# Value products and contexts on 58 columns, maxima transposed in half precision, logits copied four at a time

## The reference

```
h = layernorm(concat(emb[x], window3(pca[x]) @ proj) @ fus)
a = layernorm(h)
q, k, v = a @ Wq, a @ Wk, a @ Wv             # 16 heads of 64, biases
ctx = softmax(q k^T / 8) v
h = h + layernorm(a + ctx @ Wo + bo)
x = layernorm(h); scores = softmax(x @ wg + bg)    # 16 experts
# top 2 of 16 experts per token; per expert the best 64 of 128 positions
h = h + layernorm(x + sum_e scatter(gelu(x_e @ w1_e + b1_e) @ w2_e + b2_e))
```

## Time and profile before

| | us |
|---|---|
| median of 3 runs | 556.43 (555.6 to 559.4) |
| the profiled execution | 557.69 |
| its span, first to last instruction | 555.7 |
| TensorE busy in the span | 516.9 (93%) |
| VectorE busy | 448.6 (81%) |
| GpSimd busy | 382.2 (69%) |
| ScalarE busy | 367.2 (66%) |

### The profile page before, as it was taken

One profiled execution on the slowest core, in us unless ns is written; L12 is line 12 of the kernel. 1 busy time (PEld: TensorE's weight loads), 2 busy tenths in 40 slices (PEclk: granted clock), 3 DMA queues, 4 the chain that ended last, 5 costly groups with the idle time before them and its releaser, 6 DMA issues. The chain is left out here.

```text
span 555.7 us, 16203 instructions
## 1 busy us (share of the span) xinstructions
PE 516.9 (93%) x6063; PEld 385.9 (69%) x6063; DVE 448.6 (81%) x1013; ACT 367.2 (66%) x776; POOL 382.2 (69%) x508
## 2 busy tenths in 40 slices
PE   4996879999999999999999999878999999999874
PEld 2894757777777777777777777643457676676664
DVE  5676668888888988888888888977976988887775
ACT  1588668787877878787778778616675555555440
POOL 4000876787878878787878788942177887898783
PEclk9997999999999999999999999999999999999999
DMA  6900000000000000000000000000733044172011
GB/s 195 351 4 0 2 2 3 4 3 1 4 3 2 4 3 2 4 4 2 4 3 4 2 3 2 3 0 2 156 87 86 21 122 104 23 170 54 28 40 58
DMA packets 11905, 21.74 MB, mean 39 GB/s; under 512 B 4668, under 2 KB 9780, under 8 KB 10164
## 3 DMA queue, kind: packets, MB, share of 16 engines
q1 hardware_dynamic: 11828, 20.71, 13.6%
HBM read 16.24 MB, written 4.33 MB: 37 GB/s over the span
## 5 line engine op out<-in xcount | busy, mean ns | idle before, releaser
L792 POOL TENSOR_TENSOR s_pl<-s_pf,s_ph 128x512 f16<-128x512 f32 x128 | 147.0, 1159 | 6.9 <-ACT s_ph L890 6.7
L979 DVE TENSOR_REDUCE s_mx<-ps 128x4 f32<-128x512 f32 x128 | 83.7, 676 | 29.0 <-PE ps L1120 28.9
L770 PE MATMUL ps<-s_xt_all,s_w1s 128*128 128x512 f16 x384 | 87.8, 379 | 2.2 <-ACT s_ub L1432 1.6
L1587 PE MATMUL ps<-s_w2s,s_hid 128*128 128x256 f16 x768 | 88.9, 273 | 0.0
L884 ACT ACTIVATE s_pf<-ps 128x512 f32<-128x512 f32 x128 | 76.6, 601 | 17.3 <-PE ps L1133 17.2
L1587 PEld LDWEIGHTS ps<-s_w2s,s_hid 128*128 128x128 f16 x768 | 75.1, 98 | 10.9
L890 ACT ACTIVATE s_ph<-s_pf 128x512 f16<-128x512 f32 x128 | 77.2, 637 | 0.0
L1166 PE MATMUL ps<-s_zh,s_cth 128*128 128x256 f16 x256 | 69.8, 273 | 0.0
L1166 PE MATMUL ps<-s_zh,s_ctl 128*128 128x256 f16 x256 | 69.8, 273 | 0.0
L1166 PE MATMUL ps<-s_zl,s_cth 128*128 128x256 f16 x256 | 69.8, 273 | 0.0
L770 PEld LDWEIGHTS ps<-s_xt_all,s_w1s 128*128 128x128 f16 x384 | 37.4, 98 | 41.5 <-ACT s_ub L1432 2.1
(11 more groups left out here) (231 smaller groups left out, 1241.3 us busy)
## 6 DMA issues: line engine op xcount, KB each, us to landing
s_rep<-picks SPq DMA_DIRECT2D x14, 512.0 KB, 6.1
s_stage<-in_w SPq DMA_DIRECT2D x2, 1024.0 KB, 13.8
out<-s_ot_a SPq DMA_DIRECT2D x16, 128.0 KB, 1.7
out<-s_lg SPq DMA_DIRECT2D x16, 128.0 KB, 1.7
s_stage<-in_wq SPq DMA_DIRECT2D x1, 1024.0 KB, 5.0
s_stage<-in_wk SPq DMA_DIRECT2D x1, 1024.0 KB, 6.6
s_stage<-in_wv SPq DMA_DIRECT2D x1, 1024.0 KB, 8.3
s_stage<-in_wo SPq DMA_DIRECT2D x1, 1024.0 KB, 10.0
```

The source lines that it names most:

```text
L770: mm = nc.tensor.matmul(hidden_bank(n)[:], w1s[:, wp, c, j * P:(j + 1) * P], xt_all[:, GB * g:GB * (g + 1), xp, c, :], start=(k == 0), sto ...
L792: nc.gpsimd.tensor_tensor(flat(pl[:, b % 2, 4 * j:4 * j + 4, :]), pf[:, j, :], flat(ph[:, b % 2, 4 * j:4 * j + 4, :]), ALU.subtract).then_ ...
L979: nc.vector.tensor_reduce(mx[:, b % 2, c:c + 4], A[ab][:].rearrange("p (h k) -> p h k", h=4), AX.X, ALU.max).then_inc(max_done[hf][ab], 1)
L1587: mm = nc.tensor.matmul(zb[b % 4], hid[:, g % 2, hp, j, t * P:(t + 1) * P], w2s[:, wp, j, :], start=False, stop=(j == NJ - 1 and hp == 1))
```

## The change

- `values` multiplies only UV = 58 columns of `u` (0 to 57); `context` reads and writes only those. The six pad columns of `cn` for each head are set to zero once by VectorE, at the head of its program in this block, and TensorE's first `turn` waits for it (`cn_zero`).
- `mx` is f16, and `maxima_cols` is a matmul of f16 `mx` with an f16 identity in place of an fp32 transposition. The f16 identity, until now freed after the first block, is kept.
- `logits` of sequence b go to columns 256 + 16 (b % 4) of MISC, and `logits_out` copies the 64 columns of four sequences in the steps with i % 4 == 2. `x_cols` and `maxima_cols` wait for `lg_done` only once in four sequences.

```diff
@@ -40,6 +40,7 @@
 NJ = E * FP // P
 UD = 64
 R2, ONE, SHIFT = 2 * V, 2 * V + 1, 2 * V + 2
+UV = ONE + 1
 GB = 4
 NG = B // GB
 TAKE = S // 2
@@ -99,7 +100,7 @@
         tok = sb("h", [P, B, D])
         mvx = sb("mvx", [P, B, 2])
         lg = sb("lg", [P, B, E])
-        ident = sb("ident", [P, P])
+        ident, identh = sb("ident", [P, P]), sb("identh", [P, P], F16)
         ga1_b, ga2_b, be2_b = (sb(n, [P, D]) for n in ("ga1_b", "ga2_b", "be2_b"))
         bg_b = sb("bg_b", [P, E])
         w1s = sb("w1s", [P, 2, KC, E * FP], F16)
@@ -138,7 +139,7 @@
         ids_i, mask_i = sb1("ids_i", [P, B], I32), sb1("mask_i", [P, B], I32)
         ids_f, mask_f = sb1("ids_f", [P, B]), sb1("mask_f", [P, B])
         band, iota = sb1("band", [P, P]), sb1("iota", [P, V])
-        band16, ident16, identh = sb1("band16", [P, P], BF16), sb1("ident16", [P, P], BF16), sb1("identh", [P, P], F16)
+        band16, ident16 = sb1("band16", [P, P], BF16), sb1("ident16", [P, P], BF16)
         lhs_t = sb1("lhs_t", [P, 2 * KC, UD])
         pcaT, proj_w, proj_bT = sb1("pcaT", [20, V]), sb1("proj_w", [20, D]), sb1("proj_bT", [P, KC])
         fus_w, fus_b = sb1("fus_w", [P, 2 * KC, D]), sb1("fus_b", [1, D])
@@ -706,7 +707,7 @@
         qh, ql = sb2("qh", [P, 2, 2, 4, P], F16), sb2("ql", [P, 2, 2, 4, P], F16)
         pf = sb2("pf", [P, 4, 512])
         ph, pl = sb2("ph", [P, 2, H, P], F16), sb2("pl", [P, 2, H, P], F16)
-        mx = sb2("mx", [P, 2, H])
+        mx = sb2("mx", [P, 2, H], F16)
         mrow = sb2("mrow", [H, 2, P], F16)
         rsum = sb2("rsum", [P, 2, 8])
         cn = sb2("cn", [P, 2, 4, P])
@@ -723,7 +724,7 @@
         def sems(name, n):
             return [sem(f"{name}{k}") for k in range(n)]
 
-        rows_ready, w_hi = sem("rows_ready"), sem("w_hi")
+        rows_ready, w_hi, cn_zero = (sem(n) for n in ("rows_ready", "w_hi", "cn_zero"))
         tok_done = sems("tok_done", 3)
         shift_in = sems("shift_in", 2)
         q_ready, qhi_done, qlo_done, sm_ready, st_ready = (
@@ -988,9 +989,9 @@
                     dve.wait_ge(rs_done[hf], b + 1)
                     if b >= 1:
                         dve.wait_ge(t_ready[hf], b)
-                    nc.vector.tensor_tensor(cn[:, hf].rearrange("p t (a u) -> p (t a) u", u=UD),
-                                            CB[hf][:].rearrange("p (h u) -> p h u", u=UD),
-                                            rsum[:, hf].rearrange("p (h o) -> p h o", o=1).to_broadcast([P, 8, UD]),
+                    nc.vector.tensor_tensor(cn[:, hf].rearrange("p t (a u) -> p (t a) u", u=UD)[:, :, 0:UV],
+                                            CB[hf][:].rearrange("p (h u) -> p h u", u=UD)[:, :, 0:UV],
+                                            rsum[:, hf].rearrange("p (h o) -> p h o", o=1).to_broadcast([P, 8, UV]),
                                             ALU.mult).then_inc(cn_done[hf], 1)
 
                 def context_lo(b, hf):
@@ -1020,9 +1021,10 @@
                     nc.vector.tensor_tensor(xt_all[:, b, 1].rearrange("p c t -> p (c t)"), MISC[:, 0:D],
                                             xt_all[:, b, 0].rearrange("p c t -> p (c t)"), ALU.subtract).then_inc(xlo_done, 1)
 
-                def logits_out(b):
-                    dve.wait_ge(lg_ready, b + 1)
-                    nc.vector.tensor_scalar(lg[:, b, :], MISC[:, D:D + E], 1.0 / W_SCALE, None, ALU.mult).then_inc(lg_done, 1)
+                def logits_out(g):
+                    dve.wait_ge(lg_ready, 4 * g + 4)
+                    nc.vector.tensor_scalar(both(lg[:, 4 * g:4 * g + 4, :]), MISC[:, D:D + 4 * E], 1.0 / W_SCALE, None, ALU.mult)\
+                        .then_inc(lg_done, 1)
 
                 def token_rows(n):
                     dve.wait_ge(rows_ready, n + 1)
@@ -1033,6 +1035,7 @@
 
                 DVE_TOKENS = {(-5, 0): (2,), (-5, 1): (5,), (-5, 2): (8,), (-4, 0): (11,), (-4, 1): (14,)}
 
+                nc.vector.memset(cn[:].rearrange("p h t (a u) -> p (h t a) u", u=UD)[:, :, UV:UD], 0.0).then_inc(cn_zero, 1)
                 for i in STEPS:
                     if has(i + 5):
                         q_lo(i + 5, 1)
@@ -1061,8 +1064,8 @@
                         gate_part(dve, 2 * i - 53, early)
                     if has(i + 3):
                         sum_root(i + 3, 1)
-                    if has(i + 1):
-                        logits_out(i + 1)
+                    if has(i + 1) and i % 4 == 2:
+                        logits_out((i + 1) // 4)
                     if has(i + 2):
                         y_scaled(i + 2)
                     if has(i + 3):
@@ -1147,11 +1150,13 @@
                             c = (2 * t + ab) * UD
                             h = 8 * hf + 4 * ab + t
                             for n, (p, u) in enumerate(((ph, uh), (ph, ul), (pl, uh))):
-                                mm = nc.tensor.matmul(CB[hf][:, c:c + UD], p[:, b % 2, h, :], u[:, b, 0, :],
+                                mm = nc.tensor.matmul(CB[hf][:, c:c + UV], p[:, b % 2, h, :], u[:, b, 0, 0:UV],
                                                       start=(n == 0), stop=(n == 2))
                     mm.then_inc(pv_ready[hf], 1)
 
                 def turn(b, hf):
+                    if b == 0:
+                        pe.wait_ge(cn_zero, 1)
                     pe.wait_ge(cn_done[hf], b + 1)
                     for t in range(4):
                         tp = nc.tensor.transpose(CB[hf][:, t * P:(t + 1) * P], cn[:, hf, t, :], ident[:])
@@ -1174,8 +1179,8 @@
                 def x_cols(b):
                     pe.wait_ge(x_done, b + 1)
                     pe.wait_ge(mrow_done, min(b + 4, B))
-                    if b >= 1:
-                        pe.wait_ge(lg_done, b)
+                    if b >= 1 and b % 4 == 0:
+                        pe.wait_ge(lg_done, b // 4)
                     for c in range(KC):
                         tp = nc.tensor.transpose(MISC[:, c * P:(c + 1) * P], xc[:, b % 2, c * P:(c + 1) * P], ident[:])
                     tp.then_inc(xt_ready, 1)
@@ -1187,7 +1192,7 @@
                     n = 0
                     for c in range(KC):
                         for xp, wp in ((0, 0), (0, 1), (1, 0)):
-                            mm = nc.tensor.matmul(MISC[:, D:D + E], xt_all[:, b, xp, c, :], wgs[:, wp, c, :],
+                            mm = nc.tensor.matmul(MISC[:, D + b % 4 * E:D + b % 4 * E + E], xt_all[:, b, xp, c, :], wgs[:, wp, c, :],
                                                   start=(n == 0), stop=(n == 5))
                             n += 1
                     mm.then_inc(lg_ready, 1)
@@ -1197,9 +1202,9 @@
                         pe.wait_ge(max_done[1][n], b + 1)
                     if b >= 1:
                         pe.wait_ge(mrow_done, b)
-                    if b >= 4:
-                        pe.wait_ge(lg_done, b - 3)
-                    nc.tensor.transpose(MISC[0:H, 0:P], mx[:, b % 2, :], ident[:]).then_inc(mt2_ready, 1)
+                    if b >= 7 and b % 4 == 3:
+                        pe.wait_ge(lg_done, b // 4)
+                    nc.tensor.matmul(MISC[0:H, 0:P], mx[:, b % 2, :], identh[:], start=True, stop=True).then_inc(mt2_ready, 1)
 
                 def tokens(i, place):
                     for n in TOKENS.get((i, place), ()):
```

## The result

| | before | changed |
|---|---|---|
| median of 20 runs, us | 557.46 (554.29 to 559.4) | 554.79 (552.47 to 558.03) |
| profiled execution, us | 557.69 | 553.80 |
| span of it, us | 555.7 | 551.9 |

The ratio is 0.9954, with a 95% interval of 0.9940 to 0.9968: faster by 2.7 us by the medians, where 5.15 was forecast, and 554.79 lies outside the range of 549.9 to 554.4. The sign is right and half of the gain is missing.

What follows compares the result with a forecast made beforehand. TensorE's own column time was taken to bound the steady step. Savings of 3.48, 1.56, 0.06 and 0.05 us total 5.15: 557.69 becomes 552.5, and the median, 1.26 lower, 551.3 us; range 549.9 to 554.4.

Steps and rivals of the forecast that it cites:

- Value products, 64 to 58 columns: TensorE's value products in attention: 26.7 ns each, 2.5 less; 60 ns per set of 24, 3.48 us over 58 sets.
- The floor: Shortest spacing of short TensorE matmuls, taken as 26 ns from six 16-column logits matmuls, a little below 58 columns' 26.7.
- Rival 1: Value products stay at 29 ns despite fewer columns; only 1.7 us saved, 554.8 us; chance 0.09.
- Maxima in half precision: Maxima's transposition on TensorE, 0.11 us in fp32, takes 55.6 ns in f16; saves 54 ns per sequence, 1.56 us over 29.
- the hole behind it stays: On TensorE, the fixed gap of about 0.10 us after the maxima, where 128-row and 64-row matmuls alternate, remains.
- Contexts, logits, zeroing: VectorE work: context multiplication 50 ns less, four-sequence logits copy 220 ns, memset 0.25 us; almost all off the path.
- What is late next: At a step of 8.77 us, GpSimd's loop keeps 0.4 us of room; late maxima DMAs none or two times, ±0.7 us.
- rival 2: Another loop, GpSimd's or the half context, takes over before 8.77 us; half the gain lost, 553.9 us; chance 0.09.
- The end: Steps after 341.90 us, set by a loop with VectorE gate work: savings fall into waits, 0; possibly up to 0.4 us.
- rival 3: TensorE's granted clock falls as its waits grow; two half-clock stretches of 6.9 us give 558.2 us, slower; chance 0.04.

Runs made afterwards that it cites:

- val64: Changed kernel with value products and contexts on 64 columns again and no zeroing of pad columns; steady step 8.993 us against 8.873.
- max_f32: Changed kernel with the maxima in fp32 and transposed as before; step 8.827 us, 553.37 us, ratio 0.9921 to the kernel before.
- pad128: Changed kernel with the maxima's f16 weights zero-padded from 16 to 128 columns; step 8.777 us; 553.45 and 551.02 us, ratios 0.9932 and 0.9881 to the kernel before.
- pad128_lg1: pad128 with logits copied for each sequence, as in the kernel before; steady step 8.777 us.
- max_f16tr: Changed kernel with the maxima as an f16 transposition of 16 columns instead of a matmul; steady step 8.873 us.
- max_f32mm: Changed kernel with the maxima as an ordinary fp32 matmul of 16 weight columns; steady step 9.040 us.
- pad64: Changed kernel with the maxima's f16 weights zero-padded from 16 to 64 columns; steady step 8.893 us.

## Why the prediction missed

Of the 3.5 us between the forecast, 551.3, and 554.79, 1.0 is the base: the median of the kernel before was 556.43 over 3 runs and is 557.46 over 20. The other 2.5 are missing gain.

*Value products, 64 to 58 columns*: right to the nanosecond (26.7 ns, 0.120 us a step by val64). The floor is there, at 25 ns, just under the new width; the prediction put it at 26, and its rows give (208.51 − 208.35) / 6 = 26.7, which is too rounded to part it from the new width. Rival 1 is out by its mechanism. That its time, 554.8 us, is the measured one is chance: another term failed, and the base was higher.

*Maxima in half precision*: the step that failed, a saving of 54 ns for each sequence. "128 columns of f16 take 55.6 ns" and "the hole behind it stays" both hold, within 4 ns. The bounds, 0 and 54, left out a loss, and nothing in the argument excluded one; the row used as nearest, the query matmuls, has 128 weight columns. Against the 54 ns stands a hole of 93 ns ahead of the matmul: 50 − 93 = −43 instead of +54 a step by the distances, −46 by the steps of max_f32 and the changed kernel. With 46 the sum is 3.48 + 0.11 − 29 × 0.046 = 2.26 us, 0.41%; measured 0.46% (0.32 to 0.60). That the totals agree so well is partly luck, given the clock (below) and the spread of pad128; the distances carry the argument. So the mechanism of the forecast, a step bound by TensorE's own time, was right, and one term had the wrong sign. A sign of it stood in the earlier trace rows: holes of 0.10 us at changes of the array's shape were used as a fixed item, without asking which shape the new instruction would have.

*Contexts, logits, zeroing*: 631, 225 and 138 ns, forecast 630, 220 and 250; nothing on the path of the steady steps. Once, before the last maxima, the longer copy showed: 578 ns from the matmul before them, where pad128_lg1 and the kernel before have 527. *What is late next* (rival 2): neither loop that rival 2 names; at 8.777 us the waits for GpSimd, the half contexts and VectorE cost TensorE no time in the steady steps. The DMAs of the maxima are late in a few steps, about as forecast: in none of the changed kernel's, in two of 28 of pad128's (three are longer, by 0.84 us together), and in three of pad128_lg1's (1.4 us). In pad128 the waits for them are these, 0.3 us by matmuls and 0.7 by weight loads.

```profile
PEld ps L1137 <- DMA s_qh<-s_mrow: 0.7, 2, 0.5
...
PE ps L1137 <- DMA s_qh<-s_mrow: 0.3, 1, 0.3
```

*The end* gained nothing, as forecast. *The clock* (rival 3): a second stretch at half clock came in the filling, as it seems to in most runs of before. In five of the versions a further one of 3.4 us began between 356 and 366 us and cost 1.3 us there (26.8 to 26.9 us from sequence 28 to 31 in place of 25.5). Each such stretch takes 0.003 off the mean clock of a run. Of the changed kernel's 20 runs 8 have 0.985 or 0.986, with a median of 555.99 us against 553.94 for the other 12; of 23 runs of the kernel before only one is so low. Those runs weren't made side by side, so whether the change makes it more frequent stays open; if it does, the clock hides some 0.9 us of the gain, and rival 3 would be true in part.

## What to carry to other kernels

Before a small matmul is made cheaper, look at the shape that it gives to the array, in rows and in weight columns, beside that of its neighbours: a lone f16 matmul with 16 or 64 weight columns between full ones costs 93 ns before it and some 99 behind it, more than its own columns. Padding its weights with zeros to 96 or 128 columns cost nothing here, where the load hides beside the matmul ahead. And a bound of zero on an unknown cost needs a reason: a replaced instruction can be dearer.

## What had not been expected of the hardware

- A hole of 93 ns before a matmul with 16 or 64 weight columns (max_f16tr, max_f32mm, pad64 and the changed kernel), none with 96 or 128.
- No such hole between two narrow matmuls: in max_f32mm the second load starts 15 ns after the first.
- An fp32 transposition with 16 columns is exempt (56 ns before it, and 110 ns to the next full one), while an fp32 matmul (149 ns) and an f16 transposition (149 ns) with the same 16 are not.
- A matmul of few columns has a floor of 25 ns from start to start; 58 columns take 26.7, 64 take 29.1.
